# Expert up-projections as three fp16 products of split weights and inputs

## What is computed

```python
logits = jnp.einsum('bsd,de->bse', x, gate_w) + gate_b
probs = jax.nn.softmax(logits, axis=-1)
top_probs, top_idx = jax.lax.top_k(probs, 2)
top_probs = top_probs / jnp.sum(top_probs, axis=-1, keepdims=True)
dispatch = jnp.sum(jax.nn.one_hot(top_idx, n_experts, dtype=x.dtype) * top_probs[..., None], axis=-2)
h1 = jnp.einsum('bsd,edh->bseh', x, w1)
h2 = jnp.einsum('bsd,edh->bseh', x, w2)
hidden = jax.nn.silu(h1) * h2
expert_out = jnp.einsum('bseh,eho->bseo', hidden, w3)
return jnp.einsum('bseo,bse->bso', expert_out, dispatch)
```

## Time and profile before

| | |
|---|---|
| median of 3 runs | 1471.23 us (1469.86 to 1482.88) |
| profiled execution: its time / its span | 1470.42 us / 1468.5 us |
| mean granted clock of TensorE | 0.784 of full |
| busy: PE, DVE, ACT, POOL | 1125.3, 888.7, 505.0, 245.2 us |

### The profile page before, as it was taken

The page is one execution under the profiler, slowest core; times in us unless marked ns, Lnnn a source line. Parts: engine busy times, 40 slices in busy tenths (PEclk is TensorE's granted clock), DMA queues, the critical chain, the costliest instruction groups (busy, mean ns, idle before and its releaser), DMA issues. The chain is left out here.

```text
span 1468.5 us, 26362 instructions
## 1 busy us (share of the span) xinstructions
PE 1125.3 (77%) x9003; PEld 648.5 (44%) x9003; DVE 888.7 (61%) x2711; ACT 505.0 (34%) x1330; POOL 245.2 (17%) x359
## 2 busy tenths in 40 slices
PE   6778877677998666666666656669947999999996
PEld 2356653343555344444444444437543333333332
DVE  6686736745776555555555555551264766666665
ACT  3443423452443222222222222234404334343432
POOL 3103102000000000000000000000001444454545
PEclk9899988878999855555555555569958999999999
DMA  7000000000000000000000000000005634554540
GB/s 270 0 2 2 1 2 0 1 0 1 1 0 1 1 1 0 0 0 0 0 0 0 0 0 0 0 1 0 0 0 108 136 95 112 103 111 105 105 111 7
DMA packets 23053, 46.90 MB, mean 32 GB/s; under 512 B 1616, under 2 KB 5840, under 8 KB 22608
## 3 DMA queue, kind: packets, MB, share of 16 engines
q1 hardware_dynamic: 22992, 46.10, 13.5%
HBM read 43.47 MB, written 2.62 MB: 31 GB/s over the span
## 5 line engine op out<-in xcount | busy, mean ns | idle before, releaser
L1587 PE MATMUL wide<-ls_h,ls_v 128*128 128x16 f16 x2304 | 104.8, 176 | 172.0 <-DVE ls_h L1680 172.0
L2017 PE MATMUL wide<-xpad,w 64*128 64x512 f32 x1024 | 228.7, 596 | 3.7 <-PEq L80 3.2
L2061 DVE TENSOR_TENSOR ex_hid<-wide,ex_gated 128x1024 f32<-128x1024 f32 x128 | 156.8, 1225 | 88.9 <-ACT ex_gated L2051 87.5
L2051 ACT ACTIVATE ex_gated<-wide 128x1024 f32<-128x1024 f32 x128 | 131.2, 1025 | 202.1 <-PE wide L2017 202.1
L1587 PEld LDWEIGHTS wide<-ls_h,ls_v 128*128 128x128 bf16 x2304 | 81.6, 106 | 241.0 <-DVE ls_h L1680 241.0
L1997 POOL TENSOR_TENSOR ex_acc<-ex_part,ex_acc 128x512 f32<-128x512 f32 x120 | 152.8, 1273 | 131.5 <-DVE ex_part L2072 117.0
L2017 PEld LDWEIGHTS wide<-xpad,w 64*128 64x128 f32 x1024 | 96.7, 187 | 134.5 <-issue 124.9
L1667 DVE SCALAR_TENSOR_TENSOR ls_ig<-ls_gates 128x16 f32<-128x16 f32 x256 | 53.0, 207 | 127.1 <-ACT ls_gates L1607 127.1
L1607 ACT ACTIVATE ls_gates<-wide 128x32 f32<-128x32 f32 x256 | 50.6, 198 | 229.0 <-PE wide L1592 229.0
L2029 PE MATMUL wide<-ex_hid,w 128*64 128x512 f32 x512 | 116.7, 598 | 0.0
L2072 DVE TENSOR_TENSOR ex_part<-wide,ex_d 128x1024 f32<-128x1024 f32 x64 | 78.4, 1225 | 30.1 <-PE wide L2029 27.3
(11 more groups left out here) (339 smaller groups left out, 1860.6 us busy)
## 6 DMA issues: line engine op xcount, KB each, us to landing
ex_d<-route SPq DMA_DIRECT2D x64, 512.0 KB, 7.8
par_attn<-in_attn SPq DMA_DIRECT2D x1, 2704.0 KB, 13.3
par_rest<-in_rest SPq DMA_DIRECT2D x1, 2139.0 KB, 17.8
L_xin<-in_x SPq DMA_DIRECT2D x8, 256.0 KB, 5.9
w<-in_w SPq DMA_DIRECT2D x1, 2048.0 KB, 22.2
out<-ex_acc SPq DMA_DIRECT2D x16, 128.0 KB, 4.4
w<-in_w SPq DMA_DIRECT2D x1, 512.0 KB, 23.0
route<-ro_dt SPq DMA_DIRECT2D x8, 64.0 KB, 1.7
```

Of the source, the lines that this page charges most:

```text
L1587: pe.matmul(ig[:, g, :] if g < 2 else o, vp[part][:, g, :], h1[:], start=False, stop=False, skip_group_check=True)
L2017: mm = pe.matmul(pair_of_up(G, j)[:, h * TW:(h + 1) * TW], m.w12[r, (2 * e + w) * HID:(2 * e + w + 1) * HID], m.xn[r, t * TW:(t + 1) * TW] ...
L2051: act.activation(gated[:, n % 2, :], pair_of_up(n // GS, 2 * (n % GS))[:], ACT.Silu)\
L2061: dve.tensor_tensor(hid[:, n % (2 * GS), :], pair_of_up(n // GS, 2 * (n % GS) + 1)[:], gated[:, n % 2, :], ALU.mult).then_inc(s["hid_ready ...
```

## The change

The weights `w12` and the inputs `xn` are each split in two fp16 parts, a high one (the value rounded) and a low one (what is left), and an up becomes three products that add up in PSUM: high by high, low weights by high input, high weights by low input. A scale for the weights, a power of two from their largest magnitude, is found first; the scales are taken out again in the Silu and in `weigh`. The downs stay in fp32.

- In the recurrence VectorE reduces 256 columns of `w12` to their largest magnitude, once in 16 steps (`wtop`).
- At the start of the sigmoid attention a chain over VectorE and TensorE makes `wscale` and `unscale`; TensorE's two small matmuls of it stand ahead of the stage's first. The scores wait for `scale_ready`, and so does ScalarE's first step.
- In each of its 8 tiles ScalarE writes 512 columns of `wh` and VectorE 512 of `wl`.
- In the routing ScalarE writes `xh` and VectorE `xl` of the first tile; in the experts the other seven are written while the tile before is worked on.
- An up has six fp16 matmuls in place of two fp32 ones; Silu has a scale for each partition, and `weigh` is a `scalar_tensor_tensor`.

```diff
@@ lstm_stage, VectorE @@
+            dve.wait_ge(m.moe_landed, 32)
             with dve.Fori(0, HW // (2 * STEPS)) as i:
...
+                        if b == 1 and q == 3:
+                            dve.tensor_reduce(m.wtop[:, bass.ds(i, 1)], m.w12[:, bass.ds(i * HW, HW)], AXX,
+                                              ALU.max, apply_absolute_value=True)
@@ sigmoid_attention_stage, TensorE @@
+            pe.wait_ge(s["scale_step"], 2)
+            pe.transpose(bank[2][0:1, 0:P], top[:, 0:1], p["ident"]).then_inc(s["turned"], 1)
+            pe.wait_ge(s["scale_step"], 4)
+            pe.matmul(bank[3][:, 0:1], ones[:], top[0:1, 2:3], start=True, stop=True).then_inc(s["spread"], 1)
...
                 if attend:
                     pe.wait_ge(s["q_ready"], 2 * t + 3)
+                    pe.wait_ge(s["scale_ready"], 1)
@@ ScalarE @@
                 if attend:
                     weights(2)
                     weights(3)
+                    w = bass.ds(t * TW, TW)
+                    act.activation(m.wh[:, w], m.w12[:, w], ACT.Copy, scale=wscale[:, 0:1]).then_inc(s["wh_ready"], 1)
+
+            act.wait_ge(s["scale_ready"], 1)
@@ VectorE @@
             dve.memset(qz[:], 0.0).then_inc(s["zeroed"], 1)
+            dve.memset(ones[:], 1.0).then_inc(s["scale_step"], 1)
+            dve.tensor_reduce(top[:, 0:1], m.wtop[:], AXX, ALU.max).then_inc(s["scale_step"], 1)
+            dve.wait_ge(s["turned"], 1)
+            dve.tensor_reduce(top[0:1, 1:2], bank[2][0:1, 0:P], AXX, ALU.max).then_inc(s["scale_step"], 1)
...
+            dve.wait_ge(s["spread"], 1)
+            dve.tensor_copy(wscale[:], bank[3][:, 0:1]).then_inc(s["scale_step"], 1)
...
                     xa = tile_of(m.xa, t)
                     dve.tensor_tensor(xa, bank[k][:], xa, ALU.add).then_inc(s["out_ready"], 1)
+                    w = bass.ds(t * TW, TW)
+                    dve.wait_ge(s["wh_ready"], t + 1)
+                    dve.scalar_tensor_tensor(m.wl[:, w], m.w12[:, w], wscale[:, 0:1], m.wh[:, w], ALU.mult,
+                                             ALU.subtract).then_inc(s["wl_ready"], 1)
@@ route_stage, VectorE, behind the additions of the bias @@
+            dve.wait_ge(s["xh_ready"], 1)
+            dve.scalar_tensor_tensor(m.xl[:, 0], m.xn[:, 0:TW], XSCALE, m.xh[:, 0], ALU.mult, ALU.subtract)\
+               .then_inc(s["xl_ready"], 1)
@@ expert_stage, TensorE @@
-                for h in range(2):
-                    r = slice(C * h, C * (h + 1))
-                    mm = pe.matmul(pair_of_up(G, j)[:, h * TW:(h + 1) * TW],
-                                   m.w12[r, (2 * e + w) * HID:(2 * e + w + 1) * HID],
-                                   m.xn[r, t * TW:(t + 1) * TW], start=True, stop=True)
+                if e == 0 and w == 0 and t:
+                    pe.wait_ge(s["xh_ready"], t)
+                    pe.wait_ge(s["xl_ready"], t)
+                for n, (weight, x) in enumerate(((m.wh, m.xh), (m.wl, m.xh), (m.wh, m.xl))):
+                    for h in range(2):
+                        r = slice(C * h, C * (h + 1))
+                        mm = pe.matmul(pair_of_up(G, j)[:, h * TW:(h + 1) * TW],
+                                       weight[r, (2 * e + w) * HID:(2 * e + w + 1) * HID], x[r, t % 2, :],
+                                       start=(n == 0), stop=(n == 2))
@@ ScalarE @@
-                act.activation(gated[:, n % 2, :], pair_of_up(n // GS, 2 * (n % GS))[:], ACT.Silu)\
-                   .then_inc(s["gated_ready"], 1)
+                act.activation(gated[:, n % 2, :], pair_of_up(n // GS, 2 * (n % GS))[:], ACT.Silu,
+                               scale=m.unscale[:, 0:1]).then_inc(s["gated_ready"], 1)
+                t = n // E + 1
+                if n % E == E // 2 and t < TILES:
+                    if t >= 2:
+                        act.wait_ge(s["up2_done"], E * (t - 1))
+                    act.activation(m.xh[:, t % 2], m.xn[:, t * TW:(t + 1) * TW], ACT.Copy, scale=XSCALE)\
+                       .then_inc(s["xh_ready"], 1)
@@ VectorE @@
+                t = n // E + 1
+                if n % E == E // 2 + 1 and t < TILES:
+                    dve.wait_ge(s["xh_ready"], t)
+                    dve.scalar_tensor_tensor(m.xl[:, t % 2], m.xn[:, t * TW:(t + 1) * TW], XSCALE, m.xh[:, t % 2],
+                                             ALU.mult, ALU.subtract).then_inc(s["xl_ready"], 1)
...
-                dve.tensor_tensor(part[:, r], pair_of_down(G, r)[:].rearrange("p (e n) -> p e n", e=2),
-                                  d[:, G % GT, 2 * r:2 * r + 2, :], ALU.mult).then_inc(s["part_ready"], 1)
+                dve.scalar_tensor_tensor(part[:, r], pair_of_down(G, r)[:].rearrange("p (e n) -> p e n", e=2),
+                                         m.unscale[:, 0:1], d[:, G % GT, 2 * r:2 * r + 2, :], ALU.mult, ALU.mult)\
+                   .then_inc(s["part_ready"], 1)
```

More of the change, by code:

```diff
@@ L44 @@
 HID = 128
+XSCALE = 2.0 ** 10
 LAYOUT = {
@@ L1700, in sigmoid_attention_stage @@
         att = sb("att", [P, 4, TW])
-        names = "zeroed warm x_ready q_done q_ready xt_done xt_ready s_done att_ready v_done out_ready".split()
+        top = sb("top", [P, 4])
+        wscale, ones = sb("wscale", [P, 1]), sb("ones", [1, P])
+        names = ("zeroed warm x_ready q_done q_ready xt_done xt_ready s_done att_ready v_done out_ready "
+                 "scale_step turned spread scale_ready wh_ready wl_ready").split()
         s = {n: sem(n) for n in names}
@@ L1808, in _ @@
             dve.memset(qz[:], 0.0).then_inc(s["zeroed"], 1)
+            dve.memset(ones[:], 1.0).then_inc(s["scale_step"], 1)
+            dve.tensor_reduce(top[:, 0:1], m.wtop[:], AXX, ALU.max).then_inc(s["scale_step"], 1)
+            dve.wait_ge(s["turned"], 1)
+            dve.tensor_reduce(top[0:1, 1:2], bank[2][0:1, 0:P], AXX, ALU.max).then_inc(s["scale_step"], 1)
+            dve.wait_ge(s["scale_step"], 3)
+            dve.tensor_scalar(top[0:1, 2:3], top[0:1, 1:2], 1e-30, None, ALU.max).then_inc(s["scale_step"], 1)
+            dve.wait_ge(s["spread"], 1)
+            dve.tensor_copy(wscale[:], bank[3][:, 0:1]).then_inc(s["scale_step"], 1)
+            dve.wait_ge(s["scale_step"], 5)
+            bits = wscale[:].bitcast(mybir.dt.int32)
+            dve.tensor_scalar(bits, bits, 0x7F800000, None, ALU.bitwise_and).then_inc(s["scale_step"], 1)
+            dve.wait_ge(s["scale_step"], 6)
+            dve.tensor_scalar(m.unscale[:], wscale[:], 2.0 ** -12 / XSCALE, None, ALU.mult)
+            dve.reciprocal(top[:, 3:4], wscale[:]).then_inc(s["scale_step"], 1)
+            dve.wait_ge(s["scale_step"], 7)
+            dve.tensor_scalar(wscale[:], top[:, 3:4], 2.0 ** 12, None, ALU.mult).then_inc(s["scale_ready"], 1)
+            dve.wait_ge(s["scale_ready"], 1)
             def step(t, k, prepare, attend):
@@ L1839, in route_stage @@
         names = "warm gate_done lg_ready exp_in e_ready step d_ready dt_done "\
-                "dt_ready stored"
+                "dt_ready stored xh_ready xl_ready"
         s = {n: sem(n) for n in names.split()}
@@ L1865, in _ @@
         def _(act):
+            act.activation(m.xh[:, 0], m.xn[:, 0:TW], ACT.Copy, scale=XSCALE).then_inc(s["xh_ready"], 1)
             act.activation(top[:, 3, 0:1], p["ident"][:, 0:1], ACT.Exp).then_inc(s["warm"], 1)
@@ L1947, in expert_stage @@
         s = {n: sem(n) for n in ("warm", "up1_done", "up2_done", "gated_ready", "hid_ready", "down_done",
-                                 "part_ready", "acc_ready")}
+                                 "part_ready", "acc_ready", "xh_ready", "xl_ready")}
         d_landed = [sem(f"d_landed{q}") for q in range(GT)]
@@ L2127, in build @@
         CH = 8 * HB
+        m.wtop = c.enter_context(nc.sbuf_tensor("wtop", [P, HW // 16], F32))
+        m.unscale = c.enter_context(nc.sbuf_tensor("unscale", [P, 1], F32))
+        m.wh, m.wl = (c.enter_context(nc.sbuf_tensor(n, [P, 2 * E * HID], F16)) for n in ("wh", "wl"))
+        m.xh, m.xl = (c.enter_context(nc.sbuf_tensor(n, [P, 2, TW], F16)) for n in ("xh", "xl"))
         with nc.sbuf_tensor("xn_steps", [P, COLS + CH], F32) as xn_steps:
```

## The result

The changed kernel takes 1425.95 us (median of five runs, 1424.61 to 1435.47), the kernel before took 1478.85 us beside it (1469.86 to 1482.88): a ratio of 0.967, 95% interval 0.9632 to 0.9708 (the two medians alone give 0.964). The forecast was 1432 us, with a range of 1421 to 1447.

A forecast was written before the change was run, and what follows sets the result against it. TensorE alone was taken to set the experts' pace. The terms -54.9 + 8.3 + 3.3 + 0.4 + 3.3 + 0.7 + 0.7 = -38.2 us, against the profiled 1470.4 us, gave 1432 us, range 1421 to 1447.

The forecast's parts named there:

- The slot: Experts' ups: an fp16 matmul slot takes half the fp32 one, 0.2145 us, saving 54.9 us over 32 groups.
- Rivals B: Experts' ups: a slot of about 0.25 us, something showing between fp16 matmuls that fp32 hides; 1447.9 us, chance 0.10.
- C: Experts' ups: each fp16 load shows before its matmul, slot 0.32 us; 1502 us, chance 0.06.
- D: Whole change: fp16 slot as long as fp32's, 1585 us, or gains given back, about 1470; chance 0.04.
- The stall: Experts, up 5 of each group: TensorE waits 0.26 us for the first Silu and product, 8.3 us in all.
- Rival A: Experts: no stall, Silu no longer than now and load after a wait hidden; 1420.6 us, chance 0.10.
- The groups with `xh`: Seven expert groups: xh delays the second Silu and product, so up 7 waits 0.48 us, 3.3 us in all.
- The turn: Experts, each group: the change from row tiles to column tiles and back stays at 0.36 us.
- The start of the experts: First group: TensorE's wait for the last Silu and product grows by some 0.4 us as ups are shorter.
- Sigmoid attention: Scale chain delays the queries by 3.3 us (bounds 2.3 and 5.0, later clock rise included); last wl adds 0.7 us.
- Routing: Between the additions and the reduce: xl of the first tile is uncovered and adds 0.7 us.
- Recurrence: VectorE's reduce of 256 columns, about 0.42 us, fits in 0.51 us of idle time and is free.

The follow-up runs named there:

- e2: The changed kernel with the factor of unscale left out of the experts' Silu: 1418.83 us in one run.
- e7: The changed kernel again, unedited, beside the kernel before: 1434.29 us, ratio 0.9732.
- e9: The changed kernel a third time, unedited, beside the kernel before: 1434.20 us, ratio 0.9718.
- e4: The changed kernel without the third product, high weights by low input: 1415.24 us in one run.
- e5: The changed kernel with the first queries ahead of the scale chain's second matmul and only wh and the first attention waiting for the scale: 1433.11 us, ratio 0.972.
- e3: The changed kernel with all three products of one batch half ahead of the other half's three: 1432.41 us in one run.
- e8: The changed kernel with scale chain beside the queries, last wl and first xl later in the routing, xh one Silu earlier: 1422.23 us, ratio 0.9672.
- e1: The changed kernel with fp32 ups from unsplit weights and inputs, all splitting kept: 1482.96 us, ratio 1.0061 to the kernel before.

## Why the prediction was right, and where it was off

**The slot.** Forecast 0.2145 us, measured 0.2155. The ups fell from 6.86 to 5.17 us a group; the term of -54.9 measures 32 x 1.688 = -54.0. Rivals B, C and D fell with it. Loads of 94 ns go by while both row tiles compute, one for each tile in each slot; a load that had to wait for its own tile's matmul would make the slot an estimated 0.2155 + 0.094 = 0.31 us. The Trainium skill, "TensorE: Matmul & The Clock Gate", Part 3, says that a load overlaps only with matmuls on other rows. The trace contradicts this, and agrees with Part 2, which allows it for the background buffer. Part 1's 215.7 ns for 512 columns agrees with the trace.

**The stall.** It is where it was forecast, at up 5, behind the product (line 2113), and e2 shows its cause. It was mis-sized: 0.26 us forecast, 0.10 measured, so that 8.3 us became 3.2. Two terms were too large. The first Silu starts 0.79 us behind the first up (1247.20 to 1247.99), not 0.90. And after a wait I charged 0.15 us for semaphore and load; the product ends at 1249.20 + 1.23 = 1250.43 and the matmul starts at 1250.48, since the matmul begins 0.01 us behind its load's start (1250.47). These two are 0.21 us; TensorE was there at 3.18 us (1250.38) and not at 3.22, which gives 0.04 back. Rival A, no stall, took 8.3 and 3.3 us away; 3.2 and 1.6 (below) are there, so of these 11.6 us 4.8 were measured, which is nearer to A's nothing than to the forecast. The Silu's 1.11 us was inside the forecast of 1.10 to 1.13. The Trainium skill, "ScalarE: Activation LUTs", in the section on the hardware spline evaluator, gives some 93 ns for an operand with a scale for each partition; the trace agrees (1113 ns against 1.02 us in the earlier trace rows).

**The groups with `xh`.** 0.48 us forecast, 9.21 - 8.98 = 0.23 measured, seven times: 1.6 us instead of 3.3, for the same two reasons.

**The turn** from row to column tiles and back was to stay at 0.36 us and is 0.29: 2 us.

**The start of the experts.** +0.4 forecast, about +2.1 measured. The ups of the first two groups, which have no downs between them, took 15.0 us before, where 2 x 7.07 = 14.1 would do, and 13.8 after, where 2 x 5.40 = 10.8 would: 0.9 over became 3.0 over. The first 30 matmuls ran in part at 1.2 GHz (granted clock 0.82 in the first 2 us and 0.57 in the next 3.1, where it was 1.00 before): 5.11 us for 15 slots, which are 3.23 us at the full clock. The prediction had no term for this clock, and it is 1.9 us; the wait for the first Silus, which it had, grew too.

Together the experts gave 49.5 us where the steps said 42.9; the 6.6 us are these terms (5.1 of stall, 1.7 of `xh`, 2.2 of turn, less 0.9 of slot and 1.7 of start, which make 6.4).

**Sigmoid attention.** The queries start 3.05 us later, 3.3 forecast. The last `wl` shows (742 ns), `wh` and the other `wl` don't. The stage is 3.8 us longer in e7 and e9, 4.0 forecast. In the first profile it is 6.0 us longer, and there the late rise of the clock is seen that the prediction had as a bound. Its first scores:

```profile
1000.80 3.77 PE L1748 MATMUL wide<-sg_qz,sg_x 128*128 128x256 f32 x8 [0.69 <-ACT sg_qz L1811]
```

They start 7.02 us behind `qz`, as in e7 (995.93, shown above), and take 3.77 us instead of 1.99: from 7 to 9 us behind `qz` the granted clock was 0.50 here (1000.78 to 1002.78) and 1.00 in e7 and e9. The stage came out 2.2 us longer, the bound had up to 1.7. Why the clock rose later in this execution of the same kernel is open.

**Routing.** +0.5 us instead of +0.7; `xl` takes 682 ns and the reduce starts 0.52 us behind the additions. **Recurrence.** Free, as forecast: 460.23 before, 459.93 to 460.99 after; the reduce takes 412 ns for the 0.42 estimated and lies in idle time.

**The whole.** -38.2 us forecast from a profile of 1470.4. Measured from the recurrence on: -40.6 in the first profile, -45.1 and -44.7 in e7 and e9. So the steps gave 2.4 to 6.9 us less than was gained; in the experts alone it is the 6.6 us. The three series of the changed kernel have medians of 1425.95, 1434.29 and 1434.20 us, and the forecast of 1432 lies among them with the mechanism right. How near it lies is in part luck. The profile it was counted from is a short execution (1470.42 us, recurrence from 504.5 us on; the medians of the kernel before are 1478.85, 1474.34 and 1470.77 us), and the changed kernel's began the recurrence at 510.3, 506.1 and 511.6 us. The gain by medians scatters from 36.6 to 52.9 us.

## What to carry to other kernels

When an engine that bounds a loop gets faster, lay the latency of the ring behind it (here up, Silu, product, up) beside the new pace before trusting the sum: it gave a stall of 0.10 us at once, and took 38 of the next 55 us (e4). A helper operation on the way, such as `xh`, is best put where the ring has slack: one Silu earlier it cost nothing in five groups of seven and 0.21 and 0.26 us in two. And work that is moved ahead inside a stretch at the lower clock may run there at half the speed; of 2.7 us so moved 0.5 were left (e5).

## What the hardware showed that I had not expected

**Row tiles behave as queues of their own.** In e3 matmuls of two row tiles start in pairs every 0.2155 us although the program has three of one tile ahead of three of the other. The Trainium skill, "TensorE: Matmul & The Clock Gate", Part 3, has matmuls in strict program order from start to end; across row tiles the trace shows otherwise.

**VectorE and GpSimd.** `xl`, whose two inputs both lie in SBUF, takes 682 ns in the routing, where GpSimd idles, and 1108 to 1460 ns in the experts; the products that read one input from PSUM keep their 1223 ns. The tile view of the changed kernel (ns minimum/median/maximum), then the timeline:

```profile
L2118 DVE SCALAR_TENSOR_TENSOR xl<-xpad,xh x7: 1108/1155/1460, 1152.4 to 1369.3; 128x512 f16<-128x512 f32 x7
L1932 DVE SCALAR_TENSOR_TENSOR xl<-xpad,xh x1: 682/682/682, 1100.0 to 1100.0; 128x512 f16<-128x512 f32 x1
```

```profile
1188.12 1.27 POOL L2039 TENSOR_TENSOR ex_acc<-ex_part,ex_acc 128x512 f32<-128x512 f32 x1
...
1188.54 1.40 DVE L2118 SCALAR_TENSOR_TENSOR xl<-xpad,xh 128x512 f16<-128x512 f32 x1
```

Here `xl` ends 0.55 us behind the end of GpSimd's addition (1189.39), as if it had waited for it, and so it does, within 0.01 us, in all seven tiles of the changed kernel and all seven of e8, whatever its own length (1.11 to 1.67 us). In e1 the median of `xl` in the experts is 681 ns; its first begins at 1154.19, 0.06 us ahead of the end of an addition, and takes 0.68 us. Two others begin 0.3 and 0.4 us ahead of such an end, take 0.87 and 0.95 us, and end 0.55 us behind it. The Trainium skill, "SBUF — State Buffer", in the section on the two separate sides, has a VectorE operation with two SBUF inputs and a GpSimd operation that reads SBUF exclude each other on a shared port for the whole instruction. These rows agree, but no run here took GpSimd's additions away to show it.
